# Graph mixer: adj transposed on VectorE from a block-exchanging load, H written in tile order

## What is computed

```
H  = (adj != 0);  w = adj[first row]
Dn = 1 / (H @ w);  Be = 1 / column sums of H           # 0 where the sum is 0
conv(v, W, b) = Dn * (H @ (Be * (H.T @ (v @ W.T)))) + b
h  = layer_norm(relu(conv(x, W1, b1)), gamma, beta)
x1 = plain_layer_norm(x + conv(h, W2, b2) + x)
agg = (adj @ x1) / max(row sums of adj, 1e-6)
out = plain_layer_norm(x1 + relu(concat(x1, agg) @ WL.T))
```

## Time and profile before

| | before |
|---|---|
| median of three executions | 1166.24 us |
| span of the profiled execution (the page's only time of it) | 1165.3 us |
| TensorE busy | 1143.4 us, 98% |
| VectorE busy | 688.6 us, 59% |
| ScalarE busy | 370.2 us, 32% |
| POOL busy | 143.2 us, 12% |
| data moved | 56.77 MB |

### The profile page before, as it was taken

One profiled execution on the slowest core, in us unless ns is written; L12 is line 12 of the kernel. 1 busy time (PEld: TensorE's weight loads), 2 busy tenths in 40 slices (PEclk: granted clock), 3 DMA queues, 4 the chain that ended last, 5 costly groups with the idle time before them and its releaser, 6 DMA issues.

```text
span 1165.3 us, 18227 instructions
## 1 busy us (share of the span) xinstructions
PE 1143.4 (98%) x6560; PEld 948.4 (81%) x6560; DVE 688.6 (59%) x1783; ACT 370.2 (32%) x816; POOL 143.2 (12%) x95
## 2 busy tenths in 40 slices
PE   6799999999999999999999999999999999999998
PEld 6669798696987969779797887968789697896976
DVE  5663468634686447755478463783647735587335
ACT  4243313422234222342233331433314333044230
POOL 1102002120111102011020110201102011020100
PEclk9899999999999999999999999999999999999999
DMA  7103010130110301112001210013000130000001
GB/s 266 55 1 145 1 37 1 54 144 0 36 40 14 144 0 36 54 40 103 9 27 54 99 45 18 18 54 144 0 18 18 54 144 0 27 10 0 1 1 36
DMA packets 29316, 56.77 MB, mean 49 GB/s; under 512 B 2416, under 2 KB 19440, under 8 KB 29296
## 3 DMA queue, kind: packets, MB, share of 16 engines
q1 hardware_dynamic: 29296, 56.50, 13.5%
HBM read 48.11 MB, written 8.39 MB: 48 GB/s over the span
## 4 chain that ended last, share of the span: by engine, by line
PE 97%; DVE 1%; issue 1%; DMA 1%; SPq 0%; ACT 0%; DVEq 0%; ACTq 0%
PE bank L662 40%; PE bank L724 10%; PE bank L687 10%; PE bank L762 9%; PE bank L784 9%; PE bank L746 9%; PE bank L696 4%; PE bank L754 2%; PE bank L770 1%; DMA W1n<-in_L_gnn_W_dram 1%; DVE H L440 0%; PE bank L647 0%; DVE unread L448 0%; DVE HT L487 0%; PE bank L651 0%
## 5 line engine op out<-in xcount | busy, mean ns | idle before, releaser
L662 PE MATMUL bank<-yv,adjT 128*128 128x257 f32 x1024 | 223.3, 379 | 0.0
L662 PEld LDWEIGHTS bank<-yv,adjT 128*128 128x128 f32 x1024 | 193.6, 189 | 31.8 <-issue 3.8
L358 ACT ACTIVATE small<-mv,small 128x1 f32<-128x1 f32 x192 | 56.5, 295 | 352.1 <-DVE mv L475 256.5
L687 PE MATMUL bank<-x_hi,H 128*128 128x258 f32 x512 | 134.7, 296 | 7.3 <-DVE H L440 6.7
L480 DVE SCALAR_TENSOR_TENSOR m_lo<-bank,small,m_hi 128x256 fp32r<-128x256 f32 x128 | 61.0, 482 | 120.7 <-ACT m_hi L353 120.7
L662 PE MATMUL bank<-x_hi,H 128*128 128x256 f32 x512 | 122.6, 283 | 0.0
L662 PE MATMUL bank<-m_hi,HT 128*128 128x256 f32 x512 | 121.5, 280 | 0.0
L662 PE MATMUL bank<-x_lo,H 128*128 128x256 f32 x512 | 121.1, 280 | 0.0
L662 PE MATMUL bank<-m_lo,HT 128*128 128x256 f32 x512 | 120.8, 279 | 0.0
L746 PE MATMUL bank<-W1T,zT 128*128 128x512 f32 x256 | 120.3, 592 | 0.0
L762 PE MATMUL bank<-gW2T,xnT 128*128 128x256 f32 x512 | 119.8, 379 | 0.0
(11 more groups left out here) (75 smaller groups left out, 1676.2 us busy)
## 6 DMA issues: line engine op xcount, KB each, us to landing
raw<-in_adj_dram SPq DMA_DIRECT2D x32, 1024.0 KB, 8.9
x_in<-in_x_dram SPq DMA_DIRECT2D x8, 1024.0 KB, 6.7
out_dram<-xres SPq DMA_DIRECT2D x32, 256.0 KB, 2.1
w_row<-in_adj_dram SPq DMA_DIRECT2D x8, 512.0 KB, 3.9
W2n<-in_L_gnn_W_dram SPq DMA_DIRECT2D x1, 512.0 KB, 3.7
W1n<-in_L_gnn_W_dram SPq DMA_DIRECT2D x1, 512.0 KB, 7.8
WLn<-in_L_gnn_W_dram SPq DMA_DIRECT2D x1, 512.0 KB, 8.6
b_row<-in_L_gnn_b_dram SPq DMA_DIRECT2D x1, 256.0 KB, 15.5
```

The source lines that it names most:

```text
L358: nc.scalar.activation(std[:, i:i + 1], mv[:, which, i, 1:2], ACT.Sqrt, bias=eps_c)\
L662: last = mm(bank(stage, i)[:, 0:n_cols], lhsT, rhs, start=(k == 0 and part == 0), stop=(k == NT - 1 and part == parts - 1))
L687: last = mm(*args, start=(c == 0 and n == 0), stop=(c == NT - 1 and n == 1))
```

## The change

For graphs 1 to 7 TensorE no longer transposes adj, and ScalarE no longer copies it. Two steps stand in for that.

- **Load.** adj is loaded a second time, into adjB, which lies in raw's place. Tile t of adjB is filled by four loads of 32 partitions each (`load_adjB`), which exchange blocks between partitions and columns. Each run in memory is 256 elements. A tile is loaded once H and the masked sum have been made from raw's tile t.
- **Transpose.** `nc.vector.transpose` turns each 32x32 block within its place (`transpose_blocks`), one instruction of 128x1024 per tile, reading adjB with a step of 8 elements and writing columns t of adjT. It stands behind the moments of L's tile t, whose weights were in that part of adjT.

For this the nodes are numbered otherwise: node p*8+t is partition p of tile t, for raw, x, xres and out. The columns of adj come in memory order, so H is now written with its columns in tile order: the comparison reads raw with a step of 8 elements and writes H densely. In graph 0 TensorE's transposes stay and read raw with the same step. HT is built by rows of tiles (`build_HT_rows`), when all eight transposes are done. sum_Dn and rDn move ahead of L. In S2's chunk 0 TensorE now waits for HT's row k before each k.

```diff
             def load_graph(b, with_w=False):
-                                 adj[b, 2 * j * P:(2 * j + 2) * P, :].rearrange("(t p) e -> p t e", p=P))\
+                                 adj[b, :, :].rearrange("(p t) e -> p t e", t=NT)[:, 2 * j:2 * j + 2, :])\
+            def load_adjB(b, t):
+                rows = adj[b, :, :].rearrange("(k r t) e -> t r k e", k=NB, t=NT)
+                for a in range(NB):
+                    sp.dma_start(adjB[a * Q:(a + 1) * Q, t, :, :], rows[t, :, :, a * RB:(a + 1) * RB])\
+                      .then_inc(adjB_loaded[t], 16)
...
                     load_graph(b + 1)
+                    for t in range(NT):
+                        sp.wait_ge(H_ready, (b + 1) * NT + t + 1)
+                        sp.wait_ge(dn_ready, (b + 1) * NT + t + 1)
+                        load_adjB(b + 1, t)
...
             def build_H_tile(c, b):
-                nc.vector.tensor_scalar(H[:, c, :], raw[:, c, :], 0.0, None, ALU.not_equal).then_inc(H_ready, 1)
+                nc.vector.tensor_scalar(H[:, c, :].rearrange("p (t n) -> p t n", t=NT),
+                                        raw[:, c, :].rearrange("p (n t) -> p t n", t=NT), 0.0, None,
+                                        ALU.not_equal).then_inc(H_ready, 1)
...
+            def transpose_blocks(t, b):
+                dve.wait_ge(adjB_loaded[t], (b - 1) * (16 * NB) + 16 * NB)
+                nc.vector.transpose(adjT[:, :, t * P:(t + 1) * P],
+                                    adjB[:, t, :, :].rearrange("p k (c j) -> p j k c", c=Q)).then_inc(adjT_ready, 1)
+            def build_HT_rows(k, b):
+                dve.wait_ge(adjT_ready, (b - 1) * NT + NT)
+                nc.vector.tensor_scalar(HT[:, k, :], adjT[:, k, :], 0.0, None, ALU.not_equal).then_inc(HT_ready, 1)
...
                 if more:
+                    dve.wait_ge(q_split, b * NT + NT)
                     for c in range(NT):
                         build_H_tile(c, b + 1)
+                        sum_Dn(c, b + 1)
+                    build_rDn(b + 1)
...
                         moments("o", 2, xres[:, i, :], i, b)
+                        if more:
+                            transpose_blocks(i, b + 1)
                 if more:
                     for e in range(NT):
-                        take_rBe(e, b + 1)
-                        if e > 0:
-                            build_HT(e - 1, b + 1)
-                        take_m_lo("S1", e, b + 1, e)
-                    build_HT(NT - 1, b + 1)
-                    for c in range(NT):
-                        sum_Dn(c, b + 1)
-                    build_rDn(b + 1)
+                        build_HT_rows(e, b + 1)
+                        if e >= 1:
+                            take_rBe(e - 1, b + 1)
+                            take_m_lo("S1", e - 1, b + 1, e - 1)
+                    take_rBe(NT - 1, b + 1)
+                    take_m_lo("S1", NT - 1, b + 1, NT - 1)
...
                 for k in range(NT):
+                    pe.wait_ge(HT_ready, b * NT + max(NT // NCH, k + 1))
                     pe.wait_ge(*emptied("S1", k, b))
                     s2_step(0, k)
...
                             s1_step(e, c, b + 1)
-                        transpose_adj(e, b + 1)
```

More of the change, by code:

```diff
@@ L67, in graph_net @@
     assert NCH == 2 and NT == 8 and ND == 2 and NH == 4
+    Q = 32
+    NB = P // Q
+    RB = C // NB
+    assert RB == Q * NT
     DP = D + 2
     YP = 2 * D + 1
-    setup_fills = [1, 0, 0, 0, 0, 0, 3, 3]
-    setup_empties = [1, 1, 1, 1, 1, 1, 3, 3]
+    W_FILLS = 3
+    setup_fills = [1, 0, 0, 0, 0, 0, W_FILLS + NT, W_FILLS + NT]
+    setup_empties = [1, 1, 1, 1, 1, 1, W_FILLS + NT, W_FILLS + NT]
     bank_of, nth = {}, {}
@@ L152, in graph_net @@
         xnT, _, _ = place("xnT", [P, 2, NH, P], F32, nxt)
+        adjB, _, _ = place("adjB", [P, NT, NB, RB], F32, raw_at)
         yv, _, _ = place("yv", [P, NT, YP], F32, HT_at)
@@ L182, in graph_net @@
         raw_loaded = [sem(f"raw_loaded{n}") for n in range(NT // 2)]
+        adjB_loaded = [sem(f"adjB_loaded{n}") for n in range(NT)]
+        adjT_ready = sem("adjT_ready")
         x_loaded, w_loaded, W2_loaded, W1_loaded, WL_loaded, rows_loaded, bias_loaded, table_loaded = (
@@ L359, in root, with take_adjT @@
                   .then_inc(std_done[norm], 1)
-            def take_adjT(c, b):
+            def take_adjT(c):
                 for half in range(2):
[L364 to L368, removed]
+                    tb = TRANSPOSE_BANKS[half]
+                    act.wait_ge(bank_full[tb], W_FILLS + c + 1)
+                    nc.scalar.activation(adjT[:, half * 4:half * 4 + 4, c * P:(c + 1) * P],
+                                         banks[tb][:, :].rearrange("p (k c) -> p k c", c=P), ACT.Copy)\
+                      .then_inc(bank_empty[tb], 1)
             for c in range(NT - 1):
-                take_adjT(c, 0)
+                take_adjT(c)
             take_m_hi("S1", 0, 0, 0)
             take_m_hi("S1", 1, 0, 1)
-            take_adjT(NT - 1, 0)
+            take_adjT(NT - 1)
             for e in range(2, NT):
@@ L482, in take_m_lo, with build_HT_columns @@
                     in1=m_hi[:, e, :].bitcast(F32), op0=ALU.mult, op1=ALU.subtract), stage, e)
[L484 to L486 removed]
+            def build_HT_columns(c):
+                for tb in TRANSPOSE_BANKS:
+                    dve.wait_ge(bank_empty[tb], W_FILLS + c + 1)
                 nc.vector.tensor_scalar(HT[:, :, c * P:(c + 1) * P], adjT[:, :, c * P:(c + 1) * P], 0.0, None,
                                         ALU.not_equal).then_inc(HT_ready, 1)
+            def transpose_blocks(t, b):
[5 more added lines that the diff above has]
+                nc.vector.tensor_scalar(HT[:, k, :], adjT[:, k, :], 0.0, None, ALU.not_equal).then_inc(HT_ready, 1)
             for n in range(1, TRANSPOSE_BANKS[0]):
@@ L678, in tiled, with H_columns @@
                         one(i, k)
+            def H_columns(c, e):
+                return H[:, c, e * P:(e + 1) * P]
             def s1_step(e, c, b):
-                lhsT = H[:, c, e * P:(e + 1) * P]
+                lhsT = H_columns(c, e)
                 hi = (bank("S1", e)[:, 0:DP], lhsT, x_hi[:, c, :])
@@ L689, in s1_step, with transpose_adj @@
                     fills_bank(last, "S1", e)
-            def transpose_adj(c, b):
-                for job in (2 * c, 2 * c + 1):
-                    pe.wait_ge(*free("TA", job, b))
+            def transpose_adj(c):
+                for half, tb in enumerate(TRANSPOSE_BANKS):
+                    pe.wait_ge(bank_empty[tb], W_FILLS + c)
                     for k in range(4):
[L695 to L698, removed]
+                        cols = raw[:, c, :].rearrange("p (n t) -> p t n", t=NT)[:, half * 4 + k, :]
+                        last = nc.tensor.transpose(banks[tb][:, k * P:(k + 1) * P], cols, ident[:, :])
+                    last.then_inc(bank_full[tb], 1)
             n_side = TRANSPOSE_BANKS[0]
```

21 lines of the change are left out of this document (9 added, 12 removed).

## The result

| | before | after |
|---|---|---|
| median | 1166.38 us | 1205.49 us |
| runs, range | 4, 1166.12 to 1167.94 | 4, 1205.15 to 1205.66 |
| span of the profiled execution | 1165.3 us | 1203.8 us |

The ratio is 1.0333, with a 95% interval from 1.0318 to 1.0347: the change makes the kernel 39 us slower. The forecast was 1234 us, 68 more than before, in a range of 1148 to 1256. The direction and the mechanism hold; the size is put too high by 29 us.

What follows compares the result with a forecast made beforehand. TensorE, busy 98% of the span, was taken as the bound. Span 1165.3 + 57.4 (seven graphs) + 7 (clock) + 3.2 (graph 0) = 1232.9, with the median 0.9 above: 1234 us, range 1148 to 1256.

Steps and rivals of the forecast that it cites:

- What can be gained: TensorE's transposes in S1 removed: chunk 0 of S2 could end at 332.7 instead of 339.7, at most 7.0 us a graph.
- The transpose, 2.2 taken: VectorE in L: one transpose per tile at 2.2 us, between 0.61 and 2.46, taking the side that strided reads slow down.
- The first rival: Transposes in L dense at 1.15, H near 0.61: 1158 us, or 1145 with HT2 ahead of POOL, 1168 with H at 1.15; chance 0.27.
- H, 1.15 taken: VectorE before L: H's strided read at 1.15 us a tile, between 0.61 and 2.46; the block ends 1 us late.
- VectorE in L: With transposes a tile takes 4.37 us against TensorE's 3.47; the last transpose ends at 324.5, the last centring at 325.0.
- POOL: Behind L: POOL starts 2.4 us after the last centring and holds up HT2 and HT3; m_lo7 stands at 347.0.
- The clock, 1 a graph taken: TensorE behind its new gaps: up to 4 us at half speed, 0 to 2 us a graph, 1 taken, 7 in all.
- The seam's sum: Chunk 0 of S2 ends at 347.9 against 339.7: +8.2 us a graph, 57.4 for seven.
- Graph 0: Eight strided H tiles add 4.3 less 1.1 of waiting, 3.2 us; strided weight loads of its 64 transposes taken as 0.
- Rival 2: Behind L: HT builds escape POOL and transposes are dense, giving the full 7.0 us a graph, 1117 us; chance 0.05.
- Rival 3: Before L: H's strided read as slow as the transpose, 2.2 us; +16.6 a graph, about 1300 us; chance 0.09.
- Rival 4: adjB's loads: 1 KB pieces crawl; at 6.6 us a tile the last lands 4 us late, 1262 us; chance 0.04.

Runs made afterwards that it cites:

- e6: The changed kernel with nodes renumbered so H and the transposes read packed data, and POOL's residual waiting for all eight HT builds: 1124.29 us.
- e10: e6 with POOL's first doubling of x, in graph 0, also moved behind graph 0's HT builds: 1116.62 us.
- e1: The changed kernel with each 32x32 transpose reading adjB with step 1 instead of 8, so adjT holds wrong elements: 1154.6 us.
- e2: The changed kernel with POOL's doubling of x and adding of b2 waiting until all eight HT builds of the next graph are done: 1162.18 us.
- e8: The kernel before the change, with only POOL's doubling of x moved behind the eight HT builds: 1226.03 us.
- e11: The changed kernel with S2's first chunk in banks 6 and 7 in place of 2 and 3: 1201.20 us.
- e12: The changed kernel with H's comparison alone reading raw with step 1, so H's columns are in the wrong order: 1202.16 us.

## Why the prediction was right, and where its size was off

The range that was stated, 1148 to 1256, held a gain as well as a loss, so that 1205 lies in it says little. What can be judged is the forecast of 1234 with its own range, 1198 to 1256, and the steps behind it. Times from the start of L, whose seam decides it (before: chunk 0 ends at 57.5):

| | predicted | measured |
|---|---|---|
| H, masked sums and rDn end | 7.5 | 5.4 |
| first transpose starts | 9.5 | 8.5 |
| last transpose ends | 42.3 | 39.4 |
| m_lo0 ends | 45.3 | 42.4 |
| POOL starts | 45.2 | 42.7 |
| HT2 ends | 49.4 | 43.0 |
| HT3 ends | 54.3 | 47.0 |
| HT4 ends | 56.2, not held up | 51.9 |
| m_lo7 ends | 64.8 | 60.2 |
| chunk 0 of S2 ends | 65.7 | 62.3 |

- **What can be gained, 7.0 a graph.** Right: e6 and e10 run at 134.58.
- **The transpose, 2.2 taken.** Right: 2.07, and e1 shows that the side was chosen for the right reason. The 16-byte line of the Trainium skill (SBUF — State Buffer, Specifications) agrees with the trace: with 4 bytes of every 32 read, the transpose takes 1.7 times the dense time, and H 1.6 times (1098 against 688 ns). No run used another step, so the 16 bytes themselves are not shown. The skill's other rule (Vector Engine (DVE) Microarchitecture Reference, section 3.8), one element per cycle and lane, agrees for the dense read alone: 1.22 is the masked sum's time over as many elements. The first rival took that time for the strided read and falls. Read as a forecast for a dense transpose it does well: H at 1.15 put it at 1168, and HT2 ahead of POOL took 13 off, so about 1155 with both (an estimate from its two steps). e1 has both and came out at 1154.6.
- **H, 1.15 taken.** Right: 1.10. But "1 us late" was wrong. I set 1.15 + 1.27 for a tile and H starts every 2.15 us in the trace, since neighbouring instructions overlap. The block ended at 294.87, 1.2 us ahead of L's first tile, with nothing late.
- **VectorE in L.** The last transpose ended 2.9 us sooner than predicted: 0.9 because the first one starts sooner, 1.1 from the 2.07 in place of 2.2 (8 x 0.13), the rest from overlaps again. The period of a tile is 4.04 to 4.25, where 4.37 was taken, and TensorE brings one every 3.47.
- **POOL: the first mis-sized term.** Two HT builds were held up, as predicted, but HT3 and HT4 (2.80 and 3.73) in place of HT2 and HT3: POOL came 2.8 us behind the last centring, not 2.4, and HT2 began 0.39 ahead of it. POOL's second instruction ended 2.4 us sooner than predicted (51.4 against 53.8), and behind it one step of 1.95 fewer was left. m_lo7 so stood 4.6 us sooner, 1.7 more than the 2.9. e2 confirms the mechanism. The lock that the Trainium skill describes (SBUF — State Buffer, Who interferes with whom) agrees with 2.80 and 3.73 here, and e8 shows the case with two SBUF inputs (4.50 and 5.46).
- **A step that was missing.** S2's second product waits for bank 3, and so for m_lo3. I had S2 wait for HT3 and for m_lo7 only. e11 prices it at 0.6 a graph. Of the two gaps that I foretold ahead of S1's last products only the first came (3.26, where 4.4 was foretold); in place of the second, of 3.5, came the 4.21 inside S2.
- **The clock, 1 a graph taken.** About right in size. S1's products 6 and 7 took 5.6 us (331.96 to the next wait's start, 337.57) in place of 3.8, hidden in the waits that follow. Behind the gap TensorE ran at 0.50 until about 347, and then it was TensorE itself, not m_lo7 (end 349.7), that set chunk 0's end at 351.8; at full clock it would have followed m_lo7 by 0.9, at 350.6. So the low clock costs 1.2 of the seam's 4.8, an estimate from these rows.
- **The seam's sum.** +8.2 predicted, and 62.3 - 57.5 = +4.8 measured, with 0.3 behind it: 5.1 x 7 = 36 us, where I had 57.4 + 7 = 64. The error of 28 us is this term: 4.6 x 7 = 32 too much for m_lo7, less 0.2 x 7 = 1, as the clock cost 1.2 and not 1, and 0.3 x 7 = 2 behind the seam.
- **Graph 0.** 3.2 predicted, 2.4 measured, and e12 gives 3.3 for H's stride there. The strided weight loads of the transposes were taken at nothing, on the ground that a load might stay at its 142 ns. It does not: the 64 loads take 197 ns in the mean, against 150 in graph 0 of the kernel before (last section). That is 3.0 us of TensorE's time in all, and with 2.4 measured, less than H's stride alone, no cost of it shows in the sum.
- **Rivals 2, 3 and 4.** HT builds that escape POOL are e2 and e6, not this kernel. H at 2.2 did not happen. The loads came in time: no transpose waited.

What stays open: how near the time would have come to 1234 if HT2 had met POOL, as predicted. HT2's lead of 0.39 us was not varied by itself.

## What to carry to other kernels

Work that is moved to an idle engine must fit the gap it goes into, per tile; here 2.07 went into a gap of 1.22, while the same instruction with dense reads fits (in e1 a tile takes VectorE 3.26 us, and TensorE brings one every 3.47). When an engine becomes late, look at what meets it there: two costs that are each smaller than the gain were larger than it together, so removing either makes the change pay (by 5 to 12 us), and removing both by far the most. And an order that frees one engine (POOL behind HT) has to be tried on the kernel it is for, since in the kernel before it cost 59 us.

## What the runs showed of the hardware

- A 32x32 transpose of 128x1024 f32 takes 1216 ns on packed reads and 2067 with 32 bytes between elements; 128x128 with the stride takes 381.
- A comparison of 128x1024 f32 takes 688 ns packed and 1098 with the same stride.
- The weight loads of a 128x128 f32 transpose on TensorE take 197 ns when they read with 32 bytes between elements, and 150 on packed reads (graph 0 of the kernels after and before):

```profile
L713 PEld LDWEIGHTS bank<-ident,raw 128*128 128x128 f32 x64 | 8.5, 197 | 0.0
```
```profile
L696 PEld LDWEIGHTS bank<-ident,raw 128*128 128x128 f32 x64 | 7.9, 150 | 0.0
```

- Where a VectorE operation and a POOL instruction meet, the one that started later ends late. HT ends 0.55 us behind POOL's instruction, a masked sum 1.1 (e8). It goes the other way too: in e8 each of POOL's two starts while a masked sum runs (up to 343.10, and up to 347.64), and takes 4.51 and 5.43 where it takes 3.60 and 4.57 alone (e2), which is 0.9 more.
- Loads of 32 partitions ran at about half the rate of those over 128. At about 240 us, where raw is loaded for graph 2, nothing moves but its 4 MB, with the DMA engines full; the slices of the kernel before (4 loads of 1 MB) and of e6 (16 of 256 KB) show 418 and 216 GB/s (same columns as above):

```profile
240.00:244.00 4.00, 4.00 (x37) 4.00 (x36) 1.36 (x3) 1.31 (x3) 0.00 (x0) 1.00 1.02 418
```
```profile
241.00:245.00 4.00, 4.00 (x36) 4.00 (x35) 0.97 (x2) 0.95 (x2) 0.00 (x0) 1.00 1.03 216
```

Raw's runs in memory are 4 KB in both. The loads differ in their partitions and in their size, and no run separates the two.
